# Conv loop skewed by steps, pixel norms from the Gram diagonal and through a DRAM row, bulk loads on ScalarE's queue, and the expert gate moved ahead of U and of the second norm

## What is computed

```python
def conv(feature):                      # feature = groupnorm(x), 32 groups
    norm = sqrt(sum(feature**2, channel))
    feat_n = feature / max(norm, 1e-12)
    corr = [sum(shift(pad(feat_n), r, c) * feat_n, channel) for r, c in 28 offsets]   # 7x7 star
    return einsum(concat(feature, corr), conv_w) + conv_b       # 220 -> 192 channels
x = x + conv(groupnorm(x))
t = tokens(x)                           # 8 x 256 tokens of 192
t = t + causal_attention(layernorm(t))  # one head of 192
t = t + ffn(layernorm(t))               # 8 experts of 469, top 1, gated
```

## Time and profile before

| | |
|---|---|
| three runs | 303.17, 303.44, 304.46 us |
| the profiled execution | 305.84 us, its span 304.0 us |
| conv stage, from the first load to the last `rows` | 0.7 to 83.95 us |
| attention stage, to the first slot loaded | 84.2 to 197.2 us |
| expert stage | 197.2 to 304.0 us |
| TensorE, VectorE, ScalarE, GpSimd busy | 74%, 58%, 41%, 31% |
| TensorE share of the chain that ended last | 52% |

### The profile page before, as it was taken

The page is one execution under the profiler, slowest core; times in us unless marked ns, Lnnn a source line. Parts: engine busy times, 40 slices in busy tenths (PEclk is TensorE's granted clock), DMA queues, the critical chain, the costliest instruction groups (busy, mean ns, idle before and its releaser), DMA issues.

```text
span 304.0 us, 5067 instructions
## 1 busy us (share of the span) xinstructions
PE 226.3 (74%) x1354; PEld 205.9 (68%) x1355; DVE 176.0 (58%) x561; ACT 124.3 (41%) x255; POOL 93.6 (31%) x102
## 2 busy tenths in 40 slices
PE   1486699897418966887876742079999999999981
PEld 1376598786408866877765632058989898998971
DVE  2253643640348364876787566736767677676750
ACT  1513134621134766896776203114433333443330
POOL 2211020100000065388786855501221222221222
PEclk9999999999655878997999555559999999999997
DMA  7976721221000005234543301022322000000000
GB/s 232 365 246 207 223 70 43 80 62 51 0 2 1 0 0 181 81 123 182 206 155 114 156 26 54 27 68 74 86 70 58 26 14 17 7 22 26 17 20 0
DMA packets 15713, 25.78 MB, mean 85 GB/s; under 512 B 3879, under 2 KB 12643, under 8 KB 14672
## 3 DMA queue, kind: packets, MB, share of 16 engines
q1 hardware_dynamic: 13824, 22.40, 23.0%
q0 software_dynamic: 1872, 3.18, 3.0%
HBM read 19.50 MB, written 6.76 MB: 86 GB/s over the span
## 4 chain that ended last, share of the span: by engine, by line
PE 52%; DVE 19%; POOL 9%; issue 8%; ACT 6%; DMA 3%; POOLq 0%; DVEq 0%; SPq 0%; ACTq 0%
PE bank L1209 6%; PE bank L1185 4%; PE bank L958 4%; PE bank L960 4%; PE bank L959 4%; PE bank L962 4%; PE bank L961 4%; PE bank L972 3%; POOL wall L383 3%; PE bank L1210 3%; POOL wall L385 2%; PE bank L953 2%; DVE gst L617 2%; PE bank L1200 2%; PE bank L980 2%
## 5 line engine op out<-in xcount | busy, mean ns | idle before, releaser
L411 POOL DMA_INDIRECT out_rows<-yo,rows x23 | 22.4, 975 | 84.2 <-DVE yo L927 84.2
L383 POOL TENSOR_TENSOR wall<-stage,wall 128x940 fp32r<-128x940 f32 x8 | 17.5, 2190 | 56.4 <-ACT wall L500 47.6
L1209 PE MATMUL bank<-wall,HH 128*128 x92 | 29.4, 374 | 1.5 <-DVE HL L907 1.5
L912 DVE TENSOR_TENSOR gh<-gh,bank 128x470 f32<-128x470 f32 x23 | 14.8, 645 | 22.1 <-PE bank L962 21.2
L577 ACT ACTIVATE HH<-bank 128x512 fp32r<-128x512 f32 x23 | 13.8, 600 | 31.1 <-PE bank L1185 31.1
L1210 PE MATMUL bank<-wall,HL 128*128 x92 | 23.1, 251 | 0.0
L365 POOL DMA_INDIRECT token_rows<-rows,posi x16 | 19.0, 1188 | 9.7 <-issue 7.4
L958 PE MATMUL bank<-wall,FH 128*128 x46 | 19.7, 429 | 1.0 <-DVE FL L915 1.0
L907 DVE TENSOR_TENSOR HL<-bank,HH 128x512 fp32r<-128x512 f32 x23 | 15.9, 692 | 7.3 <-ACT HH L577 6.1
L583 ACT ACTIVATE FH<-bank 128x256 fp32r<-128x256 f32 x23 | 8.9, 385 | 24.6 <-PE bank L1200 23.2
L580 ACT ACTIVATE gh<-bank 128x470 f32<-128x470 f32 x23 | 13.0, 565 | 13.5 <-PE bank L962 13.5
(11 more groups left out here) (218 smaller groups left out, 723.5 us busy)
## 6 DMA issues: line engine op xcount, KB each, us to landing
stage<-in_w_all SPq DMA_DIRECT2D x8, 1324.0 KB, 6.4
rows<-token_rows SPq DMA_DIRECT2D x23, 98.0 KB
near_rows<-gram SPq DMA_DIRECT2D x8, 243.0 KB, 2.6
xcm<-in_x_cm SPq DMA_DIRECT2D x2, 768.0 KB, 9.4
rows<-in_x_tm SPq DMA_DIRECT2D x1, 1536.0 KB, 14.4
token_rows<-emptyt SPq DMA_DIRECT2D x9, 98.0 KB, 5.6
taps_sb<-near_rows SPq DMA_DIRECT2D x8, 103.0 KB, 2.1
small_sb<-in_small SPq DMA_DIRECT2D x1, 704.0 KB, 15.4
```

The source lines that it names most:

```text
L383: nc.gpsimd.tensor_tensor(w[:, W12:2 * W12], stage[:, par, 0:W12], w[:, 0:W12].bitcast(F32), ALU.subtract)
L411: pool.indirect_dma_start(out=out, out_offset=bass.IndirectOffsetOnAxis(ap=rows[:, j, C + 2:C + 3].bitcast(U32), axis=0), in_=yo[:, par], ...
L1209: nc.tensor.matmul(dst[:, 0:2 * C], HH[:, 1 - par, k], w(0, P, c0, c0 + 2 * C), start=(k == 0), stop=False)
```

## The change

The conv stage's order and its way to the norms are new, and the LAG goes from 3 to 4; the bulk loads move; in the attention stage two blocks swap places on TensorE and two on VectorE.

```diff
-LAG = 3
+LAG = 4
-GANGS = ((0, 2), (2, 5), (5, 8))
+GANGS = ((0, 1), (1, 4), (4, 8))
...
 # SyncE
+            load_images(1)
+            sp.dma_start(s2[:], small2).then_inc(small2_in, 16)
+            load_images(2)
             sp.dma_start(s1[:, conv0:attn0], small1[:, conv0:attn0]).then_inc(small1_in, 16)
...
+            def norms_to(b):
+                sp.wait_ge(row_ready, b + 1)
+                sp.dma_start(norms[PADDED * b:PADDED * (b + 1)].rearrange("(a n) -> a n", a=1), norm_row[0:1, b % 2]).then_inc(norms_out[b % 2], 16)
+            def norms_from(b):
+                sp.wait_ge(norms_out[b % 2], 16 * (b // 2 + 1))
...
+                window = bass.AP(tensor=norms.tensor, offset=PADDED * b, ap=[[1, REACHED], [1, PIX]])
+                sp.dma_start(rnh[0:REACHED, b % 2], window).then_inc(rnh_in[b % 2], 16)
+            for b in range(IMAGES + 1):
+                if b < IMAGES:
+                    norms_to(b)
+                if b:
+                    taps_from(b - 1)
+                if b < IMAGES:
+                    gram_to(b)
+                    norms_from(b)
...
 # GpSimd: the clamp is now its own instruction, and a mask is added
+                nc.gpsimd.tensor_scalar(ssq[:, at], ssq[:, at], EPS_NORM * EPS_NORM, None, ALU.max).then_inc(ssq_kept, 1)
                 nc.gpsimd.tensor_tensor(rn[:, at], ssq[:, at], root[:, at], ALU.pow).then_inc(rn_ready, 1)
+            def mask_norms(b):
+                pool.wait_ge(rnh_in[b % 2], 16 * (b // 2 + 1))
...
+                nc.gpsimd.tensor_tensor(rnm[0:REACHED, b % 2], rnh[0:REACHED, b % 2], c1("beside")[0:REACHED], ALU.mult).then_inc(masked, 1)
...
 # ScalarE
-            def squares(b):
-            def copy_norms(b):
-            def copy_taps(b):
+            def take_gram(b):
...
+                    ins = nc.scalar.activation(gram[:, b % 2, h, c0:c0 + NEAR], bank[4 + b % 2][:, NEAR * h:NEAR * (h + 1)], ACT.Copy, scale=rn[:, j:j + 1])
+            def take_row(b):
...
+                nc.scalar.activation(norm_row[:, b % 2, EDGE:EDGE + PIX], bank[2][0:1, c0:c0 + PIX], ACT.Copy).then_inc(row_ready, 1)
+            for i in range(IMAGES + 2):
+                if i >= 2:
+                    take_row(i - 2)
+                    take_gram(i - 2)
                 if i < IMAGES:
...
                     norm_pixels(i)
+                    high_pixels(i)
                 if i == 0:
+                    sc.dma_start(rows[:, 0:TILES, 0:C], x_tm).then_inc(tm_in, 16)
+                if i == 2:
+                    sc.dma_start(s1[:, attn0:S1N], small1[:, attn0:S1N]).then_inc(attn_in, 16)
+                if i == 3:
+                    sc.dma_start(heads, emptyt[:].rearrange("p (a c) -> p a c", a=1).to_broadcast([P, EXPERTS + 1, ROW])).then_inc(empty_out, 16)
+                if i in (4, 6):
+                    e = (i - 4) // 2
+                    sc.dma_start(stage[:, e], w_all[e]).then_inc(stage_in[e], 16)
...
 # VectorE
-            def take_squares(b):
-            def take_gram(b):
-            def spread_norms(b):
+            def pixel_squares(b):
+                ve.wait_ge(gram_ready, b + 1)
...
+                    ins = nc.vector.tensor_tensor_reduce(out=diag[:, b % LAG, h], in0=bank[4 + b % 2][:, c0:c0 + P], in1=ident, scale=1.0, scalar=0.0,
+                                                         op0=ALU.mult, op1=ALU.add, accum_out=ssq[:, HALVES * b + h:HALVES * b + h + 1])
+            def scale_taps(b):
...
+                nc.vector.tensor_tensor(tapsT[:, b % 2], bank[3][0:TAPS, 0:PIX], rnm[0:TAPS, b % 2], ALU.mult).then_inc(taps_copied, 1)
...
 # TensorE
-            def pixel_sums(b):
-            def near_norms(b):
+            def norm_rows(b):
+                pe.wait_ge(rn_ready, b + 1)
...
+                    mm = nc.tensor.matmul(bank[2][:, c0:c0 + P], rn[:, j:j + 1].to_broadcast([P, P]), ident, start=True, stop=True)
+            for i in range(1, IMAGES + LAG):
...
+                if 2 <= i < IMAGES + 2:
+                    norm_rows(i - 2)
+                if i <= IMAGES:
+                    near_gram(i - 1)
...
                 if i >= LAG:
...
+                    turn_taps(i - LAG)
                     conv(i - LAG)
                     conv_taps(i - LAG)
...
 # attention, VectorE: the gate's chain (on(t, 3)) now stands ahead of xn2 (on(t, 2));
 # TensorE: the gate's four matmuls now stand behind the scores and ahead of U
```

More of the change, by code:

```diff
@@ L96 @@
 _at = 0
-for _n, _w in (("gm", 4 * CA), ("cf", 2 * C), ("taps", C), ("place", TAPS), ("beside", P), ("one", 2), ("wq", 4 * CA), ("wk", 4 * CA), ("wv", 2 * C)):
+for _n, _w in (("gm", 4 * CA), ("cf", 2 * C), ("taps", C), ("place", TAPS), ("beside", PIX), ("wq", 4 * CA), ("wk", 4 * CA), ("wv", 2 * C)):
     S1[_n] = (_at, _at + _w)
@@ L231, in build @@
         near_out = [sem("near_out0"), sem("near_out1")]
-        taps_in = [sem(f"taps_in{k}") for k in range(LAG)]
+        taps_in = [sem("taps_in0"), sem("taps_in1")]
+        norms_out, rnh_in = [sem("norms_out0"), sem("norms_out1")], [sem("rnh_in0"), sem("rnh_in1")]
         dve = sem("dve_step")
@@ L697, in _ @@
[L697 to L711 removed]
+            link(image_stats(1, *GANGS[1]))
@@ L827, in step @@
                     nc.vector.tensor_tensor(oh[:], lg[:], gmx[:].rearrange("p (h a) -> p h a", a=1).to_broadcast(wide), ALU.is_equal).then_inc(oh_ready, 1)
+                if on(t, 2):
+                    ve.wait_ge(rs_ready, t - 1 + AHEAD)
+                    ve.wait_ge(t2t_ready, t - 2 + AHEAD)
+                    for h in range(HALVES):
+                        row = rows[:, bass.ds(2 * t + (h - 4), 1), 0:C].rearrange("p a c -> p (a c)")
+                        ins = nc.vector.tensor_scalar(xn2[:, h], row, ln2[:, h, 0:1], ln2[:, h, 1:2], ALU.subtract, ALU.mult)
+                    ins.then_inc(xn2_ready, 1)
                 if weights:
@@ L1081, in step @@
                     mm.then_inc(s_ready, 1)
+                if on(t, 3):
+                    pe.wait_ge(x2_copied, t - 2 + AHEAD)
+                    pe.wait_ge(pos_ready, t - 3 + AHEAD)
+                    wg = c2("wg")
+                    for h in range(HALVES):
+                        dst = bank[7][:, EXPERTS * h:EXPERTS * (h + 1)]
+                        nc.tensor.matmul(dst, x2T[:, 0, P * h:P * (h + 1)], wg[:, 0:EXPERTS], start=True, stop=False)
+                        mm = nc.tensor.matmul(dst, x2T[:, 1, P * h:P * (h + 1)], wg[:, EXPERTS:2 * EXPERTS], start=False, stop=True)
+                    mm.then_inc(g_ready, 1)
                 if on(t, 0):
@@ L1258, in lay_out @@
     place[len(offs), REACHED] = 1
-    px = np.arange(P) % SIDE
-    beside = (np.abs(px[:, None] - px[None, :]) <= REACH).astype(f)
-    one = np.stack([np.ones(P, f), (np.arange(P) < CB).astype(f)], 1)
-    s1 = [a_b0(cols_a_bb(gm)), a_bb(conv_w[:, :C].T), taps, place, beside, one,
+    far = np.arange(PIX)[None, :] + np.arange(P)[:, None] - EDGE
+    beside = (np.abs(far % SIDE - np.arange(PIX)[None, :] % SIDE) <= REACH).astype(f)
+    s1 = [a_b0(cols_a_bb(gm)), a_bb(conv_w[:, :C].T), taps, place, beside,
           a_b0(cols_a_bb(wq.T)), a_bb(cols_a_bb(wk.T)), a_bb(wv)]
```

274 lines of the change are left out of this document (118 added, 156 removed).

## The result

| | before | changed |
|---|---|---|
| median, us | 303.95 (4 runs, 303.17 to 304.78) | 309.22 (4 runs, 306.64 to 311.25) |
| ratio | | 1.0147, 95% interval 1.0093 to 1.0202 |
| profiled execution, its span | 305.84, 304.0 | 311.25, 309.4 |
| conv stage ends (`tri_sb` starts) | 84.2 | 93.3 |
| attention stage ends (`slot_row`) | 194.1 | 198.5 |

The change is slower by 1.5%, where I had forecast 284.0 us. The profiled execution of the changed kernel is the slowest of its four. In the two profiles the three stages part as follows: the conv stage is 9.1 us longer, not 17 shorter; the attention stage takes 105.2 us in place of 109.9; the expert stage takes 110.9 against 109.9.

The account below looks back on a forecast made before the run. No engine bounds the conv stage, but the serial chain of a middle step, 5.19 us. 305.84 minus 17.0 (conv stage) minus 2.5 (gate) is 286.3; the median lies 2.4 lower: 284.0 us, own range 280 to 289.

Parts of the forecast that it names:

- End: Conv stage from image 7's norm rows at 57.4: small transfers 2.3 us each, stage end 67.0 against 83.95.
- Loads on ScalarE's queue: Bulk loads issued by ScalarE: 0.1 us a step; slowed small transfers change little, two steps (8.2 us) against 4.6 + 0.65.
- 5.7 us for four of the small transfers, 74: Upper end of the conv stage's forecast end: four small transfers at 5.7 us, stage end 74 us.
- round trips take over: Conv stage rival: four small transfers per image in a row, each image L + 1.1; at L = 8, some 311 us; chance 0.04.
- Start: Conv stage's first part: Gram 0 at 14.8, 5.15 us a step, Gram 3 at 30.2, conv 0 ending 36.3 against 44.33.
- Middle: Conv stage's middle: TensorE without gaps from about 29, clock rise about 42, then 4.1 us a step, weight products done 56.9.
- Gate: Attention stage, choice ahead of the second norm: 0.5 us for five steps, minus 2.5; ends minus 6 and plus 3.
- Shared port: Rival: VectorE's split and choice stand still beside GpSimd, costing 9 us and the gate's 2.5; 295.5 us, chance 0.11.
- Clock stays low: Rival: TensorE stays at 1.2 GHz, convs 1 to 4 take 7.2 each, conv stage ends near 80; 297 us, chance 0.05.
- Better: Case: clock rises between 15 and 24 us, all steps 3.9, conv stage ends at 60; 277 us, chance 0.08.
- Doesn't do what it says: Rival: VectorE's wait for a conv closes the loop again, steps stay at 5.2; plus 4.5, 288.5 us, chance 0.06.

## Why the prediction was wrong

**The failed step is *End*, with the term under *Loads on ScalarE's queue* that rests on it: small transfers at 2.3 us each.** The value was taken from near_rows (2.46) and taps (2.0), both of 128 partitions; the new window read has 103, and I moved their price to it by its size in bytes. It takes 6.1 us for image 7, 4.7 of them for its packets on one engine, and it holds up the share that every other transfer has on that engine. The upper end of that term, "5.7 us for four of the small transfers, 74", stretched only the last image, where each of the eight pays. Of the 25.2 us that I was off, 23.2 are this read: with 112 rows the time is 286.06, in my own range of 280 to 289. Even there 2.3 us was too little, with medians of 3.9 for near_rows and 4.2 for the window read. The two steps that an image has from its row to its scaling hide that mostly, as I had counted. Two of the signs of being wrong that I had listed showed in the changed kernel: the window landing over 4 us, and TensorE idle for taps_sb in the middle steps.

**The rival "round trips take over" was the right mechanism, with the wrong chance.** It put an image at L + 1.1 and the stage's end at 38.5 + 7L. The row writes of images 2 to 7 are 8.52 us apart, so L = 7.4, and the formula gives 90.3, against 93.3. Its 0.04 rested on the median of 2.1 "beside two loads only". What I did not ask is what else sets a transfer's time than its bytes. L is largest beside the expert loads that ScalarE issues at 34.3 and 51.6: 11.52 and 10.39 us. There the one engine has 105 KB of window and a sixteenth of 1324 KB, 85 KB, which at 22 GB/s are 8.6 us.

**Why 5.7 in the earlier trace rows:** I read it as taps queued behind 1.3 MB of weights and took that for the reason to favour the move of the loads. That the order of issue is the cause is not shown: with the loads on ScalarE's queue a taps_sb beside one still took 6.3 us, and with them back on SyncE's queue, earlier, the longest was 3.9. The move as made is a loss of 3 to 4.5 us against SyncE's early issue. The issues on ScalarE themselves cost as forecast in the changed kernel (0.34 to 0.68 us each).

**What held.** *Start*: Gram 0 was forecast at 14.8 and started at 15.07. A step was forecast at 5.15 us and took 5.5 (the norm rows cost 1.2 in place of 0.9, the clamp beside the split 0.75 in place of 0.25). Gram 3, forecast for 30.2, came at 32.2, and conv 0 ended at 37.0 in place of 36.3. The clock rose inside conv 0, near 36 us, and made up 1.3 of the 2 us; I had put the rise at 42, so conv 0's end is near by luck. In the kernel with 112 rows the two numbers are 30.9 and 36.5, but its Gram 0 started at 13.77. The start differs by up to 1.6 us between profiles whose start has the same code (13.77 to 15.38).

*Middle*: with the loads on SyncE's queue a step took 4.3 to 4.5 us, not 4.1, and 4.0 to 4.2 once the copies were out of the loop that I had written down with 0.38 + 0.65 in it. The clock's early rise and the longer steps cancel: norm rows 7 start at 56.60 there, forecast 57.4.

*End* without the slow read: 9.6 us from there to the last add, as forecast, 66.2 against 67.0. That is luck as well. From the norm rows to the taps' landing it was 6.8 us in place of 5.7, and the rest, which I had counted at the slow clock, ran at the fast one in 2.8. My own terms for that rest (0.5, 2.2, 1.35, 0.57) make 4.6 and the stage's end 67.7; I had added them up to 67.0.

*Gate*: forecast minus 2.5, measured minus 3.0 on the time. The changed kernel itself shows why (timeline: start, us, engine, line, instruction, idle before), against the earlier trace rows:

```profile
150.26 0.70 DVE L865 TENSOR_SCALAR xn<-rows,ln 128x192 f32 x2
...
153.43 0.59 ACT L557 ACTIVATE XH<-bank 128x512 fp32r<-128x512 f32 x1
...
154.06 0.69 DVE L815 TENSOR_TENSOR XL<-bank,XH 128x512 fp32r<-128x512 f32 x1 [0.60 <-ACT XH L557]
```

The second norm no longer waits, and XL starts when XH ends; before it was 0.62 late.

**Other rivals.** *Shared port*: GpSimd's clamp takes 0.21 alone and 0.74 to 0.92 beside the split, its power 0.71 and once 1.26 (with 112 rows). A mask takes 0.73, and up to 1.25 beside VectorE's work. Collisions are there: a clamp that starts at 18.27 ends at 19.02, 0.24 behind the split that ends at 18.78, as if it had stood still until then. It is the short clamp that waits for the split, not the split for power and mask, at 0.5 us a time: some 1.6 us over the three steps from Gram 0 to Gram 3, not 9. *Clock stays low*: it rose, but in the changed kernel the stalls brought it down again (0.50 granted at 87 to 88 us, the last conv_taps, L1041, in 1.35 where it takes 0.67 at the fast clock). That is part of the cost of the slow read. *Better*: it did not come; the clock stayed slow to conv 0, and the earliest end of the conv stage in any of these kernels is 64.6. *Doesn't do what it says*: no; image order and places were as laid out.

## What to carry to other kernels

Price a new DMA by its shape first: work out over how many engines its outermost dimension can be dealt, and give each its share of the bytes at the rate that one engine shows in the trace; a read of 103 rows cost 16.6 us where one of 112 cost nothing measurable. While one slow transfer is under way, everything dealt to all engines waits for its share on that one, on whatever queue. And when a stage is shortened by cutting waits, look at TensorE's clock behind it before counting the gain: a conv stage that ended 1.8 us sooner was followed by an attention stage 2.0 us longer. Compare a single profile's times only after its start has been compared, which alone moved by 1.6 us here.

## What the runs showed of the hardware

- One DMA engine moves 21 to 23 GB/s by the windows (a packet of 1 KB every 0.042 us), all sixteen 351 at a share of 0.93. The share in a short window is enough to see how many work: 0.07 for one.
- A slow read on ScalarE's queue delayed SyncE's transfers as much as one on their own queue: near_rows 6.0 against 6.2 us median, and 3.9 where no slow read is there. Two queues took turns on the engine, packet by packet: near_rows' packets 0.084 us apart in place of 0.041.
- A one-engine read of 103 rows cost 16.6 us over eight images with 1 KB a row, some 2 with 256 bytes. Its packets took 0.042 and 0.017 to 0.019 us each, so less than in proportion to the bytes.
- A GpSimd clamp of 0.21 us took 0.58 to 0.92 beside a VectorE split, which itself stayed at 0.68 to 0.69 in all but one case (1.06).
- TensorE idle for 1.3 us ahead of image 7's taps went with a fall of its clock in one kernel, and 2.0 us ahead of image 6's in another; 0.9 and 1.5 us ahead of image 7's left it fast in two others.
